# Feed-forward and query/key products in row pairs, first loads in thirds, more products on constants, and another order of the steps

## The reference, cut to what matters

```python
h = patches @ W.T + b                                   # [1152, 192], contraction over 768
# block 1, input LN(h):
k, v, r = LN(x) @ Wk_a.T, LN(x) @ Wv_a.T, LN(x) @ Wr_a.T
x  = x + sigmoid(r) * bi_wkv(decay, first, k, v) @ Wo_a.T   # two scans over the tokens of an image
kf = square(relu(LN(x) @ Wk_f.T))                       # [1152, 768]
x  = x + sigmoid(LN(x) @ Wr_f.T) * (kf @ Wv_f.T)
# block 2, input LN(h):
q, k, v = LN(x) @ qkv_w.T + qkv_b                       # 12 heads of 16 channels, 36 tokens each
x  = x + softmax(q k.T / 4) v @ proj_w.T + proj_b
gates = top 2 of 8 of LN(x) @ w_gate
x  = x + sum over the two experts: gate * (gelu(LN(x) @ W1 + b1) @ W2 + b2)
```

## Time and profile before

| | us |
|---|---|
| median of 3 runs | 350.29 (349.79 to 350.33) |
| the profiled execution | 347.99 |
| span of its instructions | 345.8 |
| PE busy | 310.9 (90% of the span) |
| DVE busy | 196.3 (57%) |
| ACT busy | 184.0 (53%) |
| POOL busy | 83.5 (24%) |
| mean granted clock of TensorE | 0.962 of full speed |

### The profile page before, as it was taken

The page is one execution under the profiler, slowest core; times in us unless marked ns, Lnnn a source line. Parts: engine busy times, 40 slices in busy tenths (PEclk is TensorE's granted clock), DMA queues, the critical chain, the costliest instruction groups (busy, mean ns, idle before and its releaser), DMA issues.

```text
span 345.8 us, 7256 instructions
## 1 busy us (share of the span) xinstructions
PE 310.9 (90%) x2477; PEld 266.9 (77%) x2477; DVE 196.3 (57%) x524; ACT 184.0 (53%) x488; POOL 83.5 (24%) x85
## 2 busy tenths in 40 slices
PE   8988996997788899999989799996999999999980
PEld 5976783775576699779868687886998989998880
DVE  1736998799987612245474886885243334433440
ACT  1054446945584556484797897133455444555440
POOL 9710002001000201000100000013156554566532
PEclk9999999899699989999998999999899999999996
DMA  8980000000000790100769624132033233323322
GB/s 263 366 261 0 1 2 1 0 0 2 0 0 2 254 291 28 42 2 23 201 207 265 182 84 154 48 106 61 18 56 41 46 54 56 54 41 55 58 29 25
DMA packets 23296, 29.20 MB, mean 84 GB/s; under 512 B 5962, under 2 KB 18746, under 8 KB 23258
## 3 DMA queue, kind: packets, MB, share of 16 engines
q1 hardware_dynamic: 19370, 23.89, 22.6%
q0 software_dynamic: 3888, 4.81, 8.7%
HBM read 23.58 MB, written 5.11 MB: 83 GB/s over the span
## 4 chain that ended last, share of the span: by engine, by line
PE 32%; DMA 23%; DVE 20%; issue 12%; ACT 8%; POOL 1%; DVEq 1%; POOLq 1%; SPq 1%; ACTq 0%
DMA out<-ffn 20%; PE banks L1358 7%; PE banks L1359 6%; PE banks L1461 4%; PE banks L1388 3%; PE banks L1518 2%; PE banks L1506 2%; DMA patch<-in_xp 2%; PE banks L1403 2%; DMA vs<-v_scratch 2%; DVE st L1009 2%; DVE arena L1083 1%; DVE arena L1089 1%; PE banks L1489 1%; POOL rs L672 1%
## 5 line engine op out<-in xcount | busy, mean ns | idle before, releaser
L672 POOL TENSOR_TENSOR rs<-va,consts 128x4 f32<-128x4 f32 (+3 forms) x16 | 15.4, 962 | 189.8 <-DVE va L1016 106.2
L704 POOL DMA_INDIRECT out<-ffn x20 | 32.3, 1614 | 43.9 <-DVE ffn L1315 34.8
L1609 PE MATMUL banks<-arena,ffn 128*128 x240 | 42.7, 328 | 0.0
L1609 PEld LDWEIGHTS banks<-arena,ffn 128*128 128x128 f32 x240 | 38.5, 190 | 0.5 <-issue 0.2
L941 ACT ACTIVATE ffn<-banks,chans 128x128 f32<-128x128 f32 x21 | 9.6, 457 | 48.3 <-PE banks L1582 48.3
L694 POOL DMA_INDIRECT vs<-xh_scratch,ffn x21 | 21.6, 1030 | 14.9 <-DVE ffn L1282 6.6
L1461 PE MATMUL banks<-rvw,ffn 128*128 128x192 f32 x108 | 20.4, 342 | 1.5 <-ACT ffn L851 1.5
L773 ACT ACTIVATE ht<-banks,chans 128x256 f32<-128x256 f32 (+3 forms) x32 | 16.7, 589 | 8.3 <-PE banks L1403 8.1
L1461 PEld LDWEIGHTS banks<-rvw,ffn 128*128 128x128 f32 x108 | 18.9, 201 | 2.0 <-ACT ffn L851 2.0
L1403 PE MATMUL banks<-consts,xh 128*128 128x128 f32 (+1 forms) x72 | 11.4, 286 | 9.1 <-ACT xh L757 7.1
L1388 PE MATMUL banks<-arena,patch 128*128 128x192 f32 x108 | 19.1, 330 | 0.1
(11 more groups left out here) (227 smaller groups left out, 747.3 us busy)
## 6 DMA issues: line engine op xcount, KB each, us to landing
arena<-in_w SPq DMA_DIRECT2D x8, 576.0 KB, 7.6
patch<-in_xp SPq DMA_DIRECT2D x9, 384.0 KB, 6.6
arena<-in_w1a SPq DMA_DIRECT2D x8, 384.0 KB, 6.9
vs<-v_scratch SPq DMA_DIRECT2D x24, 114.8 KB
arena<-in_w1b SPq DMA_DIRECT2D x16, 96.0 KB, 5.6
out<-h SPq DMA_DIRECT2D x1, 864.0 KB, 4.3
ffn<-in_kfw SPq DMA_DIRECT2D x1, 768.0 KB, 8.1
patch<-in_b SPq DMA_DIRECT2D x1, 768.0 KB, 4.5
```

What stands on the lines that cost most here:

```text
L672: pool.tensor_tensor(RS[:, 0:n, sl], VA[:, 0:n, sl], power, ALU.pow).then_inc(rstd_ready, 1)
L704: pool.indirect_dma_start(out[:, :], bass.IndirectOffsetOnAxis(ap=IS[:, j:j + 1], axis=0), YG[j % 2], None, compute_op=ALU.add).then_inc(s ...
L1609: ins = mm(ps[:, 0:C], HST[j % 2][:, 128 * k:128 * (k + 1)], W2[:, bass.ds(e, 1), C * k:C * (k + 1)], start=(k == 0), stop=(k == HB - 1))
```

## The change

1. `side_by_side`: in `kf` and for queries and keys in `qk`, two blocks of output channels are computed together: first the 128-row product of either block, then the 64-row products of both, one on rows 0 to 63 and the other on rows 64 to 127. For that the upper rows of `HT[:, 1, :]` must hold the same 64 channels, so ACT writes that block twice for the layer norms named in `TWICE` (one more ACT instruction for each `turn` of kind `2` and `b`, eight in all); weights that meet all 128 rows get zeros there (two more memsets on POOL, one split in two).
2. `kf` is now three steps of two blocks per batch, where it was two steps of three.
3. The token weights and the patches of tile 0 are loaded in thirds, six transfers instead of two, and `tok:0` waits for each third before its two products.
4. `FILL`: 11 products on constants instead of 5 before the first turned tile of the experts, and 3 before the second.
5. Another `ORDER`. Among other things `tok:3` stands before `stats:a:0`; `kf:0:0` and then `kf:1:0` and `kf:2:0` stand around `apply:2:1`; `pt:3` and `ot:0` stand after `sc:0:1`; `base:0`, `base:1` and `base:2` stand earlier; `turn:g:1`, `stats:g:2`, `apply:g:2` stand after `pv:15`, and `turn:g:2` after `logits:1`.

```diff
-base:3 turn:g:3 logits:3
+vl:1:3 vm:0:3 sc:1:3 exp:21 s:22 ot:10 s:23 logits:0 proj:2 base:1 exp:22 exp:23 pt:12 pt:13 stats:g:1 ot:11 vm:1:3
+pv:12 pv:13 pt:14 pt:15 ot:12 ot:13 apply:g:1 pv:14 pv:15 turn:g:1 base:2 stats:g:2 apply:g:2 ot:14 ot:15 proj:3
+stats:g:3 logits:1 turn:g:2 logits:2 apply:g:3 base:3 turn:g:3 logits:3
...
-FILL = "kvr:0:0=4 kvr:0:1=3 logits:2=3 turn:g:3=5 logits:3=3 rank=6 list=14 xt:0=5"
+FILL = "kvr:0:0=4 kvr:0:1=3 logits:2=3 turn:g:3=5 logits:3=3 rank=6 list=14 xt:0=11 xt:1=3"
...
+TWICE = "2b"
...
-def kf_blocks(half):
-    return range(HB // 2 * half, HB // 2 * (half + 1))
+def kf_blocks(part):
+    return range(2 * part, 2 * part + 2)
...
-            load("tokw", TOKW, tokw)
+            for k in range(0, KP, 2):
+                sp.dma_start(TOKW[:, C * k:C * (k + 2)], tokw[:, C * k:C * (k + 2)]).then_inc(first_loaded[k // 2], 16)
+                sp.dma_start(XP[:, 0, k:k + 2, :], xp[0, :, k:k + 2, :]).then_inc(first_loaded[k // 2], 16)
...
+                        if b == 1 and step[1] in TWICE:
+                            ins = A(HT[C1:128, b, T * tiles[0]:T * tiles[-1] + T], ps[0:rows, 0:T * len(tiles)], ACT.Identity,
+                                    bias=chan_(b_, b), scale=chan_(w, b))
...
+            def side_by_side(dst, moving, stationary, jobs):
+
+                for ps, st in zip(dst, stationary):
+                    mm(ps, st[0], moving[0], start=True, stop=False)
+                for i, (ps, st, job) in enumerate(zip(dst, stationary, jobs)):
+                    r = slice(C1 * i, C1 * (i + 1))
+                    end(mm(ps, st[1][r], moving[1][r], start=False, stop=True), job)
...
-                    for m in kf_blocks(step[1]):
-                        ps = begin(("kf", g, m))
-                        end(over_channels(ps[:, 0:T * len(tiles)], h_(T * tiles[0], T * tiles[-1] + T), w_(KFW, 128 * m, 128 * (m + 1))), ("kf", g, m))
+                    blocks = kf_blocks(step[1])
+                    ps = [begin(("kf", g, m))[:, 0:T * len(tiles)] for m in blocks]
+                    side_by_side(ps, h_(T * tiles[0], T * tiles[-1] + T), [w_(KFW, 128 * m, 128 * (m + 1)) for m in blocks],
+                                 [("kf", g, m) for m in blocks])
```

More of the change, by code:

```diff
@@ L130 @@
 ORDER = """
[L131 to L140, removed]
@@ L146 @@
-logits:0 vm:0:3 ot:10 pt:12 apply:g:1 pt:13 base:0 proj:2 stats:g:2 ot:11 turn:g:1 vm:1:3 pv:12 pv:13 pt:14 pt:15
-ot:12 ot:13 apply:g:2 pv:14 pv:15 turn:g:2 ot:14 ot:15 proj:3 stats:g:3 logits:1 logits:2 apply:g:3 base:1 base:2
-base:3 turn:g:3 logits:3
+tok:0 tok:1 tok:2 tok:3 stats:a:0 apply:a:0 tok:4 tok:5 stats:a:1 apply:a:1 turn:a:0 kvr:0:0 turn:a:1 kvr:0:1 kvr:1:0
+kvr:1:1 wkv:0:0 sub:0:0 sub:0:1 wexp:0:0 wexp:0:1 wkv:0:1 sub:0:2 wexp:0:2 sub:0:3 wkv:0:2 wexp:0:3 wkv:0:3 tok:6
+wexp:0:4 tok:7 tok:8 wkv:0:4 wkv:0:5 stats:a:2 kvr:2:1 stats:a:3 kvr:2:0 apply:a:2 apply:a:3 turn:a:2 turn:a:3
@@ new lines @@
+wexp:0:5 wkv:0:6 rc:0 wkv:0:7 kvr:0:2 kvr:0:3 wkv:1:0 kvr:1:2 wkv:1:1 wo:0 hx:0 kvr:2:3 wo:1 hx:1 wkv:1:2 sub:1:0
+sub:1:1 wexp:1:0 wexp:1:1 stats:2:0 kvr:1:3 wkv:1:3 sub:1:2 sub:1:3 wexp:1:2 wexp:1:3 wexp:1:4 apply:2:0 turn:2:0
+kvr:2:2 wexp:1:5 wkv:1:4 wkv:1:5 kf:0:0 stats:2:1 apply:2:1 kf:1:0 kf:2:0 wkv:1:6 rc:1 wkv:1:7 rv:0 rv:1 turn:2:1 wo:2
+ff:0 hx:2 wo:3 hx:3 stats:2:2 stats:2:3 apply:2:2 apply:2:3 kf:0:1 kf:1:1 kf:2:1 stats:b:0 turn:2:2 turn:2:3 apply:b:0
+turn:b:0 rv:2 rv:3 kf:0:2 kf:1:2 kf:2:2 ff:1 stats:b:1 vt:0 apply:b:1 turn:b:1 rv:4 qk:0 spread:0:0 spread:1:0 rv:5
@@ new lines @@
+kf:0:3 kf:1:3 kf:2:3 ff:2 stats:b:2 sc:0:0 sc:1:0 s:0 s:1 s:2 exp:0 vl:0:0 exp:1 exp:2 apply:b:2 s:3 exp:3 s:4 s:5
+exp:4 exp:5 rv:6 rv:7 rv:8 turn:b:2 pt:0 pt:1 vt:1 vl:1:0 vm:0:0 qk:1 spread:1:1 spread:0:1 ff:3 stats:b:3 apply:b:3
+vt:2 turn:b:3 pv:0 pv:1 pt:2 sc:0:1 s:6 s:7 exp:6 s:8 s:9 sc:1:1 vl:0:1 s:10 exp:7 vm:1:0 qk:2 exp:8 s:11 pt:3
+spread:0:2 spread:1:2 ot:0 ot:1 exp:9 exp:10 exp:11 pv:2 pv:3 vl:1:1 vt:3 ot:2 vm:0:1 vm:1:1 sc:0:2 s:12 s:13 s:14
+sc:1:2 exp:12 pt:4 qk:3 pt:5 ot:3 spread:0:3 s:15 s:16 s:17 pv:4 pv:5 proj:0 base:0 spread:1:3 exp:13 pt:6 pt:7
@@ new lines @@
+stats:g:0 exp:14 exp:15 exp:16 exp:17 ot:4 ot:5 pv:6 pv:7 vl:0:2 sc:0:3 s:18 s:19 s:20 s:21 vm:0:2 pt:8 pt:9 ot:6
+exp:18 vl:1:2 ot:7 exp:19 exp:20 pv:8 pv:9 vm:1:2 proj:1 vl:0:3 pt:10 pt:11 apply:g:0 ot:8 ot:9 pv:10 turn:g:0 pv:11
+vl:1:3 vm:0:3 sc:1:3 exp:21 s:22 ot:10 s:23 logits:0 proj:2 base:1 exp:22 exp:23 pt:12 pt:13 stats:g:1 ot:11 vm:1:3
+pv:12 pv:13 pt:14 pt:15 ot:12 ot:13 apply:g:1 pv:14 pv:15 turn:g:1 base:2 stats:g:2 apply:g:2 ot:14 ot:15 proj:3
+stats:g:3 logits:1 turn:g:2 logits:2 apply:g:3 base:3 turn:g:3 logits:3
@@ L327, in build @@
         patch_loaded = [sem(f"patch_loaded{t}") for t in range(TILES)]
+        first_loaded = [sem(f"first_loaded{i}") for i in range(KP // 2)]
         bank_full = [sem(f"bank_full{b}") for b in range(NBANK)]
```

45 lines of the change are left out of this document (25 added, 20 removed).

## The result

The changed kernel takes 354.63 us (median of 4, 353.93 to 356.02) beside 350.31 us for the kernel before on the same chip (349.79 to 351.20): ratio 1.0126, interval 1.0087 to 1.0164. It is slower by 1.3%; 348.6 was forecast, and the time is outside the range. The profiled execution took 354.25 us with a span of 352.05, 6.26 more than the span of before.

A forecast was written before the change was run, and what follows sets the result against it. Bounds by stretch: DVE's scans from 30 to 117 us, PE from 120 to 171, three engines to 197, PE in the experts' loop. Terms summed to -1.7 us: 346.3 profiled, 348.6 as median; range 345.5 to 351.5 (8 in 10).

The forecast's parts named there:

- the order elsewhere: Term for steps moved in the new order: -0.5 us around the scores of group 1, +1.0 at the stage's end.
- Pairs: `kf` and `qk` on PE: nine groups overlap fully but pay 0.32 us each for changing rows; -1.8 us.
- Overlap by one record: Rival on the pairs: the second product overlaps only one record of the first; 351.0 us at most, chance 0.09.
- overlap without a fixed part: Rival on the pairs: full overlap with no row-change cost, saving 4.7 us instead of 1.8; 345.7 us, chance 0.14.
- Second copy: Eight more ACT instructions, 4.7 us of ACT, mostly covered by other PE work; the last, `turn:b:3`, exposed; +0.5 us.
- The slower rival: Rival on the second copy: PE or DVE waits for each of ACT's eight copies, +4.2 us more; 352.8 us, chance 0.12.
- `kf` in threes: Batch 0: four blocks instead of three behind `apply:2:1` on ACT delay the table load and DVE's wait; +0.6 us.
- Thirds: First loads: tile 0's gain is lost at tile 1, and patches 1 is issued 1.86 us later, mostly absorbed; +0.1 us.
- The rival with the whole delay in issue: Rival on the first loads: patches 1 arrive later by their whole delay in issue; 350.35 us, chance 0.08.
- Fillers: More products on constants before the first gathered tiles keep the clock up; the gain reaches the end; -1.6 us.
- Order: `pt:3` and `ot:0` behind `sc:0:1` let group 1's scores, then DVE and ACT, start sooner; -0.5 us.
- tail: End of the stage before the gathers: DVE gets more work between its last `pv` and `proj:3`; +1.0 us.

The follow-up runs named there:

- e11: As e13, but both 64-row products of each pair on rows 0 to 63, so that they cannot overlap: 351.92 us, 1.0171 of the kernel before.
- e5: The changed kernel measured again, unaltered, in later rounds: 353.36 us, 1.0104 of the kernel before.
- e6: The changed kernel with the old order in the first 122 steps (the front), new order behind them (the back): 352.29 us, 1.0105 of the kernel before.
- e12: The changed kernel with eight products on constants on PE before `pv:8`: 352.38 us, 1.0165 of the kernel before.
- e9: The kernel before with only the new order and the `kf` in three steps that it needs: 351.15 us, 1.0132 of the kernel before.
- e13: The kernel before plus row pairs, second copy and `kf` in three steps; old order, whole first loads, old fillers: 348.45 us, 0.9960 of the kernel before.
- e17: The kernel before plus only ACT's eight second copies: 359.22 us, total not comparable because tokens are routed otherwise.
- e14: As e13, but `kf:1:0` ahead of `apply:2:1`: 348.26 us, 0.9989 of the kernel before.
- e10: The kernel before with only the new fillers: 348.78 us, 0.9954 of the kernel before.
- e15: The kernel before with only `kf` cut into three steps of two blocks: 348.60 us, 1.0018 of the kernel before.

## Why the prediction was wrong

The forecast was -1.7 us and +4.3 came. Three steps carry the miss: "the order elsewhere" costed a few of the moves and left out the one that cost most, the fillers' gain was taken as kept "because the loop cannot absorb it", and a later issue of patches 1 was taken to mean "less time behind" the loads ahead.

- **Pairs, -1.8.** The mechanism was right: full overlap plus a fixed part per group. Overlap by one record falls (e11), and so does overlap without a fixed part. The size was off twice. The fixed part is 0.20 + 0.20 = 0.40, not the 0.32 that I took from the earlier trace rows, so the nine groups save 3 x 0.03 + 3 x 0.25 + 3 x 0.08 = 1.1. That arrives in the new order: from the scans' end to score step 6, 61.76 to 61.90 (changed, e5, e6, e12) against 62.95 in e9. In the old order 0.4 of it is lost to ACT's wait (e13), and the last copy takes the rest up to that mark. I had called PE "the chain without a break" and so counted each PE us in full. The Trainium skill, "TensorEngine Tiling (Array Packing)", section "Tiling Modes", says that a change of mode drains the engine; the trace agrees, and gives it a price, 0.20 us each way.
- **Second copy, +0.5.** In the old order the mechanism was right, down to the step: the copy of `turn:b:3` delays the scores of group 1 by 0.68 (e17), and all others are covered. In the changed kernel this one is covered too. The slower rival, each copy on the path, was wrong.
- **`kf` in threes, +0.6.** Right: 1.51 for 1.05, +0.44, in e13, and undone in e14.
- **Thirds, +0.1.** Wrong: +1.6. I held that later issue "mostly means less time behind" the loads ahead. The loads ahead are just what is late too, since the thirds move 1.55 MB in the first 8 us where whole loads move 1.97. The rival with the whole delay in issue, at 0.08, had about this size.
- **Fillers, -1.6.** The gain arrived (-1.3 on average), but in the profiles the loop gave it back (+1.7). The step that failed is "the loop cannot absorb it": I took PE's busy share, 87.77 of 89.0, for the bound, where the page's own chain ran through the additions' landing.
- **Order, -0.5, and tail, +1.0.** The tail costs 1.0, as I had it. The gain of 0.5 is there too, where I put it: from the scans' end to score step 6 e9 takes 62.95 and e10 and e15 63.44. (At the mark `rv:8` it already looks like 0.54, but there 0.44 of it are the four transposes of `turn:b:2`, which the new order has behind `rv:8`; in e15 they stand ahead of it.) The sign was lost on what I did not cost: `wexp:0:5` behind `turn:a:3` and a new wait of 0.15 at 50.81, together +0.96. Between 30 and 117 us I costed only `kf` around `apply:2:1`, though the diff moves dozens of steps and this is DVE's chain with waits for ACT. To it come some 1.0 before `pv:8`, which may be chance, and the clock: about 1.0 in the scans in four of the seven kernels with the new front, 1.5 to 2.8 behind `pv:8` in four of the seven with the new back. My clause on what would make it wrong named both, a wait in 171 to 197 us and the clock elsewhere, but gave them no term and no chance.

By averages over the profiles, new against old: start +1.6, scans +2.2 (against 77.6), scans' end to `pv:8` -0.7, `pv:8` to the last logits +2.1, first gather to last addition +0.4, in sum +5.6. The chips gave +4.3 and, in e5, +3.5. Each profile is one execution, so the shares are known to about 1 us, and that of the clock, net of the falls that the old order has elsewhere, stays open.

## What to carry to other kernels

An order moved around a chain has to be costed move by move on the engine that the chain waits for, and even a small ACT instruction put right in front of a table load counts almost in full (0.81 of 0.92 us). A busy share of 98% is not a bound: look at what the chain of waits names there, before a gain ahead of it is counted. Time lines with fixed marks over many kernels resolve 0.1 us, where the clock is full and no transfer is waited for, and medians with 10 us of spread don't resolve 1. A step that moves across a mark looks like a gain there, and a clock fall has to be counted over kernels, at every place, not read from one.
